# Second transformer layer: the MLP's second product one turn later, and its transposes moved from TensorE to VectorE and transfers

## The reference, cut to what matters

```python
for i in range(DEPTH):
    x = x + self_attention(layer_norm(x, ln1_g[i], ln1_b[i]), Wq[i], Wk[i], Wv[i], Wo[i], bo[i])
    h = layer_norm(x, ln2_g[i], ln2_b[i])
    x = x + (gelu(h @ W1[i] + b1[i]) @ W2[i] + b2[i])
```

## Time and profile before

| | |
|---|---|
| time, median of 3 runs | 3123.52 us (3122.75 to 3123.99) |
| time of the profiled execution | 3120.52 us |
| its span in the profile | 3118.7 us |
| mean granted TensorE clock | 0.979 of 2.4 GHz |
| TensorE busy | 2921.5 us (94% of the span) |
| VectorE busy | 1676.6 us (54%) |
| ScalarE busy | 1415.3 us (45%) |
| GpSimd busy | 827.9 us (27%) |
| this layer's turns | about 718 to 2466 us of the span |

### The profile page before, as it was taken

How to read it: one execution, slowest core, us unless ns; L and a number is a source line. 1 busy time by engine, 2 the same in 40 slices (tenths; PEclk the granted TensorE clock), 3 DMA queues, 4 the chain that set the end, 5 groups by cost and what they waited for, 6 DMA issues and landing times. The chain is left out here.

```text
span 3118.7 us, 53260 instructions
## 1 busy us (share of the span) xinstructions
PE 2921.5 (94%) x20742; PEld 1958.5 (63%) x20742; DVE 1676.6 (54%) x5013; ACT 1415.3 (45%) x3117; POOL 827.9 (27%) x829
## 2 busy tenths in 40 slices
PE   6889999888999999999999999999999788799998
PEld 3566666664666666565666666665656444468887
DVE  4677776755655545545445444456555478641112
ACT  3666666633445354444444453544444134132224
POOL 1001111113323322322323223233333310025552
PEclk8999999999999999999999999999999899899999
DMA  4111111002000112010211000110100000023325
GB/s 140 18 19 19 18 19 19 13 3 72 25 28 18 38 31 69 28 55 28 67 47 35 21 14 28 32 55 20 38 20 25 11 1 28 27 68 80 75 84 189
DMA packets 102249, 126.48 MB, mean 41 GB/s; under 512 B 12451, under 2 KB 79014, under 8 KB 100960
## 3 DMA queue, kind: packets, MB, share of 16 engines
q1 hardware_dynamic: 93168, 102.56, 11.4%
q0 software_dynamic: 7680, 16.32, 2.1%
q10 hardware_dynamic: 1152, 4.19, 0.3%
HBM read 75.56 MB, written 43.61 MB: 38 GB/s over the span
## 5 line engine op out<-in xcount | busy, mean ns | idle before, releaser
L1435 PE MATMUL bank<-h2T,w 128*128 128x512 f32 x1024 | 478.8, 606 | 5.2 <-ACT gT L1373 3.7
L1473 PE MATMUL bank<-w,gT 128*128 128x256 f32 x2048 | 465.9, 381 | 0.0
L1473 PEld LDWEIGHTS bank<-w,gT 128*128 128x128 f32 x2048 | 379.3, 190 | 49.7 <-issue 0.5
L1090 POOL TENSOR_TENSOR prob<-prob,rsum 128x512 f32<-128x512 f32 (+1 forms) x256 | 237.9, 950 | 592.4 <-DVE rsum L1245 592.4
L1435 PEld LDWEIGHTS bank<-h2T,w 128*128 128x128 f32 x1024 | 182.2, 190 | 223.8 <-issue 173.6
L1373 ACT ACTIVATE gT<-bank,vec 128x512 f32<-128x512 f32 x256 | 175.1, 687 | 285.5 <-PE bank L1435 284.0
L609 ACT ACTIVATE y<-y,least 128x128 f32<-128x128 f32 (+3 forms) x512 | 252.0, 554 | 50.6 <-DVE least L479 50.6
L479 DVE CUSTOM_DVE_ANT_0 y<-bank,mask 128x128 f32<-128x128 f32 (+3 forms) x512 | 223.9, 485 | 70.2 <-PE bank L706 68.9
L1222 DVE CUSTOM_DVE_ANT_0 prob<-bank,mask 128x256 f32<-128x256 f32 (+1 forms) x512 | 164.3, 387 | 168.3 <-PE bank L1425 168.3
L1336 ACT ACTIVATE prob<-prob,least 128x256 f32<-128x256 f32 (+1 forms) x512 | 239.6, 471 | 15.8 <-DVE least L1222 15.5
L1251 DVE COPY probT<-bank 128x1024 f32<-128x1024 f32 (+1 forms) x128 | 138.4, 1082 | 189.7 <-PE bank L1489 189.7
(11 more groups left out here) (328 smaller groups left out, 5050.2 us busy)
## 6 DMA issues: line engine op xcount, KB each, us to landing
turned_rows<-score SPq DMA_DIRECT2D x124, 128.0 KB, 2.3
score<-turned_rows SPq DMA_DIRECT2D x31, 512.0 KB, 3.6
w<-in_W SPq DMA_DIRECT2D x8, 1024.0 KB, 7.6
expert_parts<-zeros SPq DMA_DIRECT2D x8, 1024.0 KB, 6.1
we<-in_we SPq DMA_DIRECT2D x16, 512.0 KB, 5.0
rows<-modulation SPq DMA_DIRECT2D x40, 128.0 KB, 3.5
x<-in_x SPq DMA_DIRECT2D x8, 512.0 KB, 6.3
prob<-score SPq DMA_DIRECT2D x64, 64.0 KB, 2.3
```

What stands on the lines that cost most here:

```text
L1090: nc.gpsimd.tensor_tensor(two, two, rsum[:, at:at + 2].unsqueeze(2).to_broadcast([P, 2, width]), ALU.mult).then_inc(s["probs"], 1)
L1435: ins = nc.tensor.matmul(M[m % 2][:, :], w1[:, k, m * P:(m + 1) * P], h2T[:, k, :], start=(k == 0), stop=(k == KD - 1))
L1473: ins = nc.tensor.matmul(M[i][:, (t % 2) * D:(t % 2 + 1) * D], gT[:, m, t * P:(t + 1) * P], w2[:, m, :], start=(m == 0), stop=(m == MF - 1))
```

## The change

The layer is spread over three turns and TensorE's transposes of the second norm and of the probabilities go:

- On TensorE, turn `g` now holds the attention of `g`, `hidden` of `g - 1` and `down` of `g - 2`. `down` stands in four pieces between the scores and the linear heads; seven of the eight pieces of `hidden` stand between `linear_out` and `values`, the eighth behind `values`.
- The second norm's output takes the way of the first: VectorE transposes squares (`turn_rows`), SP stores four groups to DRAM and reads them back (`move_rows2`), ScalarE writes `h2T` from that.
- The probabilities are transposed by VectorE in squares of 32 by 32 (`turn_probs`, four a turn) into `prob_blocks`, and SP puts the squares in place with 32 transfers from SBUF to SBUF a turn (`move_probs`, 16 for query blocks 0 and 1, 16 for 2 and 3). VectorE's four copies L1251 go.
- SP's order in a turn: the second norm's rows of g - 1, the probabilities of g, the first norm's rows of g + 1. Weight loads and the clearing of a DRAM buffer (now 32 pieces of 256 KB for 8 of 1024 KB) are put elsewhere in that order.
- The loop has 34 passes instead of 33; GpSimd's and VectorE's work on the last batches moves by one pass.

```diff
-            def move_turned1(g):
-                turned1.wait(sp, g)
+            def move_rows(away, done, arrived):
+                for i in range(GROUPS):
+                    src = rblocks[SQUARE * i:SQUARE * (i + 1), :, :, :].rearrange("p a t r -> p a (t r)")
+                    sp.dma_start(by_group[i], src).then_inc(away.sem, 16)
+                away.wait(sp, done)
+                sp.dma_start(xT, by_feature).then_inc(arrived.sem, 16)
+
...
+            def move_probs(g, h):
+                sp.wait_ge(s["probs_turned"], 4 * g + 2 * h + 2)
+                if g:
+                    sp.wait_ge(s["av_full"], g)
                 for i in range(GROUPS):
...
+                    for a in range(GROUPS):
+                        src = pblocks[h][SQUARE * i:SQUARE * (i + 1), a, :, :].rearrange("p k r -> p (k r)")
+                        dst = probT[h][SQUARE * a:SQUARE * (a + 1), i, :, :].rearrange("p k r -> p (k r)")
+                        sp.dma_start(dst, src).then_inc(probs_in[h].sem, 16)
...
-            for g in range(TURNS):
+            for g in range(TURNS + 2):
...
+                if g < TURNS:
+                    move_probs(g, 0)
+                    move_probs(g, 1)
+                if 0 < e < DEPTH and b == 1:
                     sp.wait_ge(s["w2_full"], 2 * B * e)
                     load_w2(e)
...
+                if B <= g < B + parts // 2:
+                    clear(2 * (g - B))
+                    clear(2 * (g - B) + 1)
...
+            def turn_rows(norm, count):
+                dve.wait_ge(s[norm], count)
+                nc.vector.transpose(out=rblocks.rearrange("p a t r -> p t a r"),
                                     in_=xn[:, :, :].rearrange("p t (a f) -> p t a f", f=SQUARE))\
-                  .then_inc(turned1.sem, 1)
+                  .then_inc(s["rows_turned"], 1)
+
+            def turn_probs(g, q):
+                n = len(keys_of(q))
+                first = block_of(q, 0, 0)[1]
+                dve.wait_ge(s["probs"], 8 * g + 2 * q + 2)
+                if g and q % 2 == 0:
+                    probs_in[q // 2].wait(dve, 16 * GROUPS ** 2 * g)
+                src = prob[:, 4 * q:4 * q + 4, from_col(q):PAIR]
...
+                nc.vector.transpose(out=pblocks[q // 2][:, :, first:first + 4 * n, :].rearrange("p a k r -> p k a r"),
+                                    in_=src).then_inc(s["probs_turned"], 1)
...
+                    masked(g, (0, 1))
                     linear_mid(g)
-                    masked(g, (0, 1))
+                    invert(g, 0)
                     masked(g, (2, 3))
+                    invert(g, 1)
                     if g + 1 < B:
                         modulate(g + 1)
                     if last >= 0:
                         modulate(B + last)
                     context_sum(g)
-                    invert(g, 0)
+                    turn_probs(g, 0)
+                    invert(g, 2)
+                    turn_probs(g, 1)
+                    if g >= 2:
+                        mlp_sum(g - 2, 0)
+                    invert(g, 3)
+                    if g >= 2:
+                        mlp_sum(g - 2, 1)
+                    turn_probs(g, 2)
+                    turn_probs(g, 3)
                     if g + 1 < TURNS:
                         nxt = c.y[:, (g + 1) % B]
                         if g + 1 < B:
...
+                        turn_rows("norm1", g + 2)
...
+                    turned2_in.wait(act, 16 * g)
+                    gains_in(g - 1, h2T, 2 * KD, "h2_gain")
+                if g < TURNS:
+                    exps(g, 3)
+                if g:
                     v = vec[:, (g - 1) // B, :]
                     for m in range(MF):
-                        act.wait_ge(s["hidden_full"], m0 + m + 1)
+                        if m == 2 and g < TURNS:
+                            linear_away(g)
+                        if m == EARLY and g < TURNS:
+                            values_away(g)
+                        act.wait_ge(s["hidden_full"], MF * (g - 1) + m + 1)
                         nc.scalar.activation(gT[:, m, :], M[m % 2][:, :], ACT.Gelu,
                                              bias=v[:, 4 * KD + m:4 * KD + m + 1]).then_inc(s["gelu_done"], 1)
...
+                else:
+                    linear_away(g)
+                    values_away(g)
+                if g + 1 < TURNS:
+                    turned1_in.wait(act, 16 * (g + 1))
+                    gains_in(g + 1, hT[:, :, 1:1 + T], 0, "h1_gain")
...
-            def probs_turn(g, q):
-                if q >= 2:
-                    pe.wait_ge(s["pt_out"], 4 * g + q - 1)
-                else:
-                    pe.wait_ge(s["score_min"], 16 * (g + 1))
-                keys = keys_of(q)
-                for j in range(4):
-                    if j % 2 == 0:
-                        pe.wait_ge(s["probs"], 8 * g + 2 * q + j // 2 + 1)
-                    for m in range(len(keys)):
-                        col = from_col(q) + m * P
-                        ins = nc.tensor.transpose(S[:, 2 * (q % 2) + m, j * P:(j + 1) * P],
-                                                  prob[:, 4 * q + j, col:col + P], c.ident[:, :])
-                ins.then_inc(s["pt_full"], 1)
-
             def values(g):
-                pe.wait_ge(s["pt_out"], 4 * g + 3)
                 for q in range(4):
-                    if q == 3:
-                        pe.wait_ge(s["pt_out"], 4 * g + 4)
+                    if q % 2 == 0:
+                        probs_in[q // 2].wait(pe, 16 * GROUPS ** 2 * (g + 1))
                     keys = keys_of(q)
                     for m, key in enumerate(keys):
                         for j in range(4):
+                            part, k = block_of(q, m, j)
                             ins = nc.tensor.matmul(S[32 * j:32 * j + 32, 0, q * P:(q + 1) * P],
                                                    tok[:, key, 2 * P + 32 * j:2 * P + 32 * j + 32],
-                                                   probT[:, q, m, j * P:(j + 1) * P],
+                                                   probT[part][:, :, k, :],
                                                    start=(m == 0), stop=(m == len(keys) - 1),
...
-            for g in range(TURNS + 1):
-                mlp, attn = g > 0, g < TURNS
+            for g in range(TURNS + 2):
+                attn, down_of, hidden_of = g < TURNS, g >= 2, 1 <= g <= TURNS
                 if attn:
                     project(g)
-                if mlp:
-                    pe.wait_ge(s["norm2"], g)
-                    for half in range(KD):
-                        if g >= 2:
-                            pe.wait_ge(s["w2_added"], 2 * (g - 2) + half + 1)
-                        turn(half, "turn2_full")
+                if down_of:
+                    down(g - 2, 0, 4)
                 if attn:
                     pe.wait_ge(s["lin_out"], g + 1)
                     pe.wait_ge(s["qk_out"], 2 * (g + 1))
                     scores(g, (0, 1))
-                if mlp:
-                    pe.wait_ge(s["w1_loaded"], 16 * ((g - 1) // B + 1))
-                for m in range(MF):
-                    if mlp:
-                        hidden(g - 1, m)
-                    if attn:
-                        if m == 0:
-                            linear_turn(g)
-                        if m == 2:
-                            pe.wait_ge(s["score_min"], 16 * g + 8)
-                            scores(g, (2, 3))
-                        if m == 3:
-                            pe.wait_ge(s["lin_k_ready"], g + 1)
-                            context(g)
-                if mlp:
-                    pe.wait_ge(s["w2_loaded"], 16 * ((g - 1) // B + 1))
+                if down_of:
+                    down(g - 2, 4, 12)
+                elif attn:
+                    idle_products(c, 4, 7)
+                if attn:
+                    pe.wait_ge(s["score_min"], 16 * g + 8)
+                    scores(g, (2, 3))
+                if down_of:
+                    down(g - 2, 12, 17)
+                if attn:
+                    linear_turn(g)
+                    pe.wait_ge(s["lin_k_ready"], g + 1)
+                    context(g)
+                if down_of:
+                    down(g - 2, 17, NT * MF)
+                elif attn:
+                    idle_products(c, 4, 7)
                 if attn:
                     pe.wait_ge(s["qlT_out"], g + 1)
-                    if not mlp:
-                        idle_products(c, 7, 7)
                     linear_out(g)
-                pieces = NT * MF
-                at = 0
-                for q, upto in enumerate((10, 17, 24, pieces)):
-                    if mlp:
-                        down(g - 1, at, upto)
-                        at = upto
-                    elif q in (1, 2):
-                        idle_products(c, 1, 7)
-                    if attn:
-                        probs_turn(g, q)
+                if hidden_of:
```

(39 more changed lines are left out.)

186 lines of the change are left out of this document (82 added, 104 removed).

## The result

The changed kernel takes 3324.9 us (median of 4 runs, 3322.3 to 3330.8) where the kernel before takes 3123.2: 1.065 times as long (95% interval 1.063 to 1.067). Slower was forecast, by the mechanism that the profile shows, but at 3252 us. The range ended at 3325, 1.0645 times the 3123.5 before; the measured ratio of 1.0648 is just beyond it, and the loss of 202 us is half as much again as the 129 forecast.

The account below looks back on a forecast made before the run. TensorE was taken to bound the kernel before, SP's issuing the changed one. Turn 0 +11, turns 1 to 6 +27, 7 to 26 +42, 27 to 31 +25, `W2` +16, end +8: +129, so 3252 us; range 3090 to 3325.

Parts of the forecast that it names:

- TensorE's saving: TensorE loses 8 + 28 transposes, 4.1 us a turn; if it stayed busy, a turn would be 49.5 us.
- The first transfer at 25.9 us: First half of the probabilities is ready for SP's transfers 25.9 us after the start of `project`.
- The issue at 0.616 us: SP issues the 32 probability transfers at 0.616 us each, 19.7 us in all, done at 45.6 us.
- The wait before `values`, 6 us: TensorE, ready at 41.5 us, waits some 6 us every turn for the last probabilities, landing at 47.3.
- The low clock, 1.6 us: TensorE's work behind the wait before `values` runs at a lower clock: +1.6 us, a turn of 55.7 us.
- SP's way and TensorE's end together: Without the clock, SP's way to the next turn's rows and TensorE's way both end at 54 to 54.5 us.
- The turns with `modulate`: In turns 0 to 6 and 27 to 31 `modulate` ahead of `context_sum` delays the first half by 2.4: 58.1 us a turn.
- The end, +8.3: After the last `out_proj`, 44.6 us pass instead of 36.3: +8.3.
- `W2` between the transfers, 16 us: In three turns `W2` is issued between the probabilities and the next `project`'s rows, 5.3 us charged each: +16.
- turn 0: The first turn follows the same chain through SP: 55 us for 44.2, +11.
- rival A: SP's issuing of the probability transfers is the chain, at 0.58 to 0.66 us each: 3252 us; chance 0.50.
- rival D: The DMA queue fills: landings later than 2.3 us, issues up to 0.7, +2.7 a turn, 3338 us; chance 0.12.

Follow-up runs that it names:

- the idle products: The changed kernel with six idle products of 0.92 us in TensorE's wait before the second part of `values`: 3344.0 us, 1.069 times the kernel before.
- the kernel with 16 transfers: The changed kernel with the same bytes in 16 transfers of 112 KB a turn, issued once all four blocks are turned: 3158.0 us, 1.009 times the kernel before.

## Why the prediction was right in kind and too small

- **TensorE's saving**: right, a little low. 4.1 us a turn forecast, and 53.5 - 48.6 = 4.9 measured. 3.1 of it is the step from 51.7 us, with the probabilities' transposes on TensorE, to 48.6. The rest is the second norm's 0.97 and some 0.75 that the forecast lacked: `values` and `out_proj` take 1.67 and 3.45 us to the next start for 1.96 and 3.91 before.
- **The first transfer at 25.9 us**: right, 26.2 in the turns without `modulate`, except behind the `W2` turns (below).
- **The issue at 0.616 us**: the kind was right, the size low. A row of 32 took 20.15 to 21.5 us, 20.85 on average, for 19.7 forecast: 0.652 each, 1.15 us a turn or 37 us in all. Two things make the difference. The first issue of a row is cheaper, 0.51 us, and each further one starts 0.633 behind the last; the eight of the earlier trace rows have the same shape, (4.93 - 0.51) / 7 = 0.63, and the prediction spread the cheap first one over eight where the row has 32. That alone gives 20.15, the shortest rows. The rest are single long issues: in turn 8 one takes 1.49 us where the others take 0.59, and the longest in the trace takes 1.91. They don't come of the length of the row, for the rows of 16 last 10.0 to 11.2 us. The kernel before had them too, in the same line L323 for its other target, which the earlier trace rows doesn't show. What causes them stays open.

```profile
L323 SPq DMA_DIRECT2D probT<-score x64: 507/589/1432, 32.5 to 547.9; - x64
```

- **The wait before `values`, 6 us**: right (6.1), in the place named.
- **The low clock, 1.6 us**: it was 8.6 us from the end of the wait to `project` in turn 8, for 6.7 at full speed: 1.9. How long it lasts differs: the piece of `hidden` behind the wait takes 2.6 to 3.8 us in turns 7 to 26, and with the length of SP's row that is most of why ordinary turns differ. As a part of the sum it holds only together with SP's way, as the idle products showed: removing it alone moved the wait and saved nothing.
- **SP's way and TensorE's end together**: right, shown by the idle products. In turn 8 of the changed kernel ScalarE has written `hT` 0.5 us before `project` starts.
- **The turns with `modulate`**: the mechanism right, the size low. Turns 2 to 6 began their transfers at 29.4, for 28.3 forecast, 6 us in all. In turns 27 to 31 they began at 31.0 to 32.0, for 28.8, which is 15 us. There `stats_x` stands ahead of `masked` and takes 3.0 us, 1.2 of them for an addition that it doesn't make in the first turns; in these turns it doesn't wait for GpSimd. So the second scores waited up to 2.0 us for VectorE. I had charged 0.5 for this. Against it, the forecast counted from 53.6 us a turn where these turns took 54.9 before, which hides 6.5 us of the miss.

```profile
2451.46 1.15 PE L1481 MATMUL bank<-kT,qT 32*128 32x256 f32 x16 [2.00 <-DVE least L1276]
```

- **The end, +8.3**: it was +13.4. The last `hidden` waited 5.10 us for VectorE's `mlp_sum`, which the change leaves behind `stats_x` and `modulate` there; here `stats_x` did wait for GpSimd, 3.4 us:

```profile
2637.47 15.67 PE L1493 MATMUL bank<-h2T,w 128*128 128x512 f32 x32 [5.10 <-DVE y L1251]
```

- **`W2` between the transfers, 16 us**: about right, but only in part in the place named. Those three turns are 61.0, 61.6 and 60.5 us for 57.5 in ordinary ones, 11 us; `project` waits 2.4 to 3.9 us for `hT` behind them. Behind that wait it runs in part at the low clock, 8.8 us for 7.0 in the row below (turn 10), so the turns that follow start their transfers at 28.0 to 29.2 us and last 58.8 to 60.6, another 7 us.

```profile
1313.23 8.80 PE L1464 MATMUL bank<-wtok,hT 128*128 128x512 f32 x16 [3.15 <-ACT hT L1393]
```

The step that failed is a term of the sum, as the prediction put it "I take **0.616**": the issue measured 0.652 on average over a row, which is 37 of the 73 us missed. The two smaller terms of `modulate` and the end miss 6 + 15 and 5 us, and the wrong base of the last turns takes 6.5 back. The other 16 or so are small terms: 3 in turn 0, 2 in the loads of `W2`, and in the ordinary turns a first transfer 0.3 us late and some 0.4 us more behind the wait, against a landing 0.2 us quicker. The mechanism is rival A's. That the time came near rival D's 3338 is not for D's reason: the transfers land after 2.0 us, not later than 2.3, and the median issue is 0.59 us.

By the Trainium skill (DMA: Bandwidth & Descriptors, Issuing engines are not separate DMA queues) the time to initiate a transfer is usually small beside the transfer. Here a transfer lands 1.8 to 2.0 us after its issue, and 0.59 of that is the issue itself, with 16 KB as with 64; 32 of them hold the queue for 21 us in a turn of 57. For many small transfers in a row this case disagrees.

## What to carry to other kernels

Many small transfers on one queue cost by their number, not by their bytes: 32 x 0.65 us here, and whatever is queued behind them, here the next turn's input, pays as well. Count the issues of a stage against the slack of what waits for them. Here 16 that could start at 26 us into the turn fit without a wait, 32 didn't, and the two kernels differ by 8%; 16 that could start only at 32 us didn't fit either. When the price of an issue is read from a short row, keep the cheap first one apart. When two ways end at the same moment, shortening either one alone shows nothing, so an experiment that saves nothing doesn't prove its target free.

## What the runs showed of the hardware that I had not expected

- An SBUF to SBUF transfer of 32 partitions takes SP 0.59 us to issue in a row (median) whether it carries 16, 48, 64 or 112 KB; the first of a row takes 0.51, and starts lie 0.633 apart. Single issues take up to 1.9 us.
- A second engine that issues transfers at the same time didn't help here: the landing of the 64 KB transfers went from 2.0 to 2.4 us, and ScalarE's own stores landed after 3.0 us where SP's took 2.3. Whether the limit is SP or something behind it stays open; no run issued the 32 from two queues.
- In the kernel with 16 transfers, waits before `values` of up to 2.7 us left the clock of the work behind them up (turns 7 to 26). Waits of 3.0 to 4.0 us in its turns 1 to 6 brought it down for a part of that work: `values` took 2.2 to 3.2 us for 1.7. Behind 6.1 us the granted clock was 0.50 over the next 4.4 us. Behind a wait of 3.15 us `project` took 8.8 us for 7.0.
